# Sharing the last weighted additions of an expert layer among three engines, with larger load pieces

## The chip, the cores and the metric

The kernel runs on one core of a Trainium2 chip. The metric is the device time of one execution in microseconds. Three executions of the kernel before took 713.89, 716.54 and 720.88 us; the median is 716.54 us.

## The reference

Four layers run over 16 batches of 128 tokens with 256 features, all in float32; each adds its result to `x`:

```
x = x + long_convolution_attention(layernorm(x), ctx)      # L0_xattn
x = x + dense_plus_top2_low_rank_experts(layernorm(x))     # L0_ffn
x = x + cross_attention_16_heads_quantized(layernorm(x), ctx)   # L1_xattn
x = x + moe(layernorm(x))                                  # L1_ffn
```

Only the last one matters here. It routes every token to K = 4 of 32 experts and adds a shared expert:

```
scores = sqrt(softplus(flat @ router_w.T))
_, idx = top_k(scores + expert_bias, 4)
topv   = take(scores, idx); topv = topv / (sum(topv) + 1e-20)
probs  = zeros(T, E) with topv at idx
out    = sum over experts e of probs[:, e] * swiglu_e(flat)
out    = out + shared_swiglu(flat)
x      = x + out
```

So each token's output is its `x`, plus the shared expert's row, plus four expert rows, each with a weight of its own.

## The kernel before, in words

`build` writes one program for each engine: `tensor_program`, `vector_program`, `scalar_program`, `gpsimd_program` and `sync_program` (which issues most DMAs). Up to the routing, each program is one loop over ticks; the tables `T_PE`, `T_DVE` and so on say at which tick each step of each batch stands in the program. Nothing of that is touched by the change.

**Routing.** For each token and each of its four experts, the token's normalized row is scattered by GpSimd (L1318) into `expert_rows` in DRAM, sorted by expert. A row is 260 floats: 256 values and, in column 256, the number of the row of `y_rows` where the expert's result has to go. These numbers come from the array `dest`, made on the host: before, `512 + 2048 * k + 128 * b + p` for the k-th expert of token p of batch b.

**Expert loop.** NT = 95 tiles of 128 sorted rows go through a software pipeline. SyncE loads the tile (L1393), TensorE transposes it (L598, L599), multiplies it by the gate and up weights (L610), VectorE clamps and multiplies (L990, L992, L997), ScalarE does tanh and the copies out of PSUM (L1221, L1226, L1231, L1236), TensorE multiplies by the down weights (L583), and GpSimd scatters the 128 result rows of 1 KB into `y_rows` (L1328). GpSimd counts each landed scatter up in `s_st`; its loop ends with the waits for the landings of the last three scatters. A token's four experts are numbered so that k = 3 is the one whose tile comes first, and k = 0 the one that comes last.

**Weighted additions.** At the end every token's four rows come back. In `sync_program` (L1398 to L1406), 16 loads of 512 KB each read the rows of four batches for one k: m = 0 to 3 are the four groups of four batches for k = 3, m = 4 to 7 for k = 2, and so on. Each group g has one buffer `rb[g]`. Before the first load of a round SyncE waits until all tiles of that k have landed (`s_st` against `last[k]`), and from the second round on before each load until the four additions that read this buffer are done (`s_fin`, L1404). In DRAM a load reads 1 KB for each partition and batch:

```
o = DUMP + NB * 128 * k + 512 * g
sp.dma_start(rb[g], Yr[o:o + 512, :].rearrange("(b p) d -> p b d", p=128)).then_inc(d_r[g], 16)
```

VectorE does all 64 additions in the same order after its expert loop (L1044 to L1054): `xs[:, b, :] += rb[g][:, i, :] * weight`, as one scalar_tensor_tensor of 128x256. The weights `pk4` are made during the expert loop. ScalarE and GpSimd have nothing to do after their expert loops.

**Output.** After the 16 loads SyncE issues the 16 stores of 128 KB, batch by batch, each when the batch's last addition is done (L1410), then waits for all of them.

Of the kernel before, what the change touches and what calls it, by code (L numbers as in the profile page):

```python
# [10 lines left out]
ALU = mybir.AluOpType  # L11
ACT = mybir.ActivationFunctionType
AX = mybir.AxisListType

NB = 16
NE = 32
KT = 4
# [13 lines left out]
OFF = {}  # L31
# [22 lines left out]
SD = 32  # L54
NR = 14
DUMP = 512
NX = 12
WR = 16
NW = -(-NT // 4)
# [36 lines left out]
def build(nc, a_x, a_ctxT, a_tk, a_pack, a_qp, a_rows, a_w, a_dest, a_pad, out):  # L96
    ctx = ExitStack()
    with ctx:
        def sb(name, shape, dt=F32):
            return ctx.enter_context(nc.sbuf_tensor(name, shape, dt))  # L100

        def sem(name):
            return ctx.enter_context(nc.semaphore(name))

        xs = sb("xs", [128, NB, 256])
        tk = sb("tk", [128, 16, 256])
        pk = sb("pk", [128, NPACK])
# [17 lines left out]
        def cutter(base):  # L125
            used = [0]

            def carve(shape, dt=F32):
                n = int(np.prod(shape[1:])) // (2 if dt == BF16 else 1)
                v = base[0:shape[0], used[0]:used[0] + n]  # L130
                used[0] += n
                assert used[0] <= base.shape[1], used[0]
                if dt == BF16:
                    v = v.bitcast(BF16)
                if len(shape) == 3:
                    v = v.rearrange("p (a b) -> p a b", a=shape[1])
                if len(shape) == 4:
                    v = v.rearrange("p (a b c) -> p a b c", a=shape[1], b=shape[2])
                return v
            return carve  # L140
# [33 lines left out]
        rb = [carve([128, 4, 256]) for _ in range(4)]  # L174
        cmp_ = rb[0][:, 0, 0:NE * Q].rearrange("p (q e) -> p q e", e=NE)
        cmd_ = rb[0][:, 1, 0:NE * Q].rearrange("p (q e) -> p q e", e=NE)
        carve = cutter(tk[:, 8:16, :].rearrange("p a b -> p (a b)"))
        th = [carve([128, 2, 128]) for _ in range(3)]
        hT = [carve([128, 128]) for _ in range(2)]
# [42 lines left out]
        key = sb("key", [128, NB, 8])  # L222
        ixl = sb("ixl", [128, NB, KT], U32)
        stage = sb("stage", [128, NS, ROW])

        carve = cutter(tk[:, 6:8, :].rearrange("p a b -> p (a b)"))
        scan = carve([128, 2, NE])
# [8 lines left out]
        pk4 = tk[:, 5, 192:256].rearrange("p (b k) -> p b k", k=KT)  # L236
# [5 lines left out]
        Yr = nc.dram_tensor("y_rows", (DUMP + KT * NB * 128, 256), F32, kind="Internal").ap()  # L242

        d_in = [sem(f"d_in{g}") for g in range(len(LOADS))]
# [9 lines left out]
        d_r = [sem(f"d_r{i}") for i in range(4)]  # L254
        s_tm, s_t5, s_thr, s_x5P, s_x5 = (sem(n) for n in ("s_tm", "s_t5", "s_thr", "s_x5P", "s_x5"))
        d_xr = [sem(f"d_xr{i}") for i in range(2)]
        d_out = sem("d_out")

        v_own, p_own, a_own = (sem(n) for n in ("v_own", "p_own", "a_own"))
        s_const, s_pconst, s_st = (sem(n) for n in ("s_const", "s_pconst", "s_st"))  # L260
# [26 lines left out]
        po = ctx.enter_context(nc.psum_tensor("po", [128, 512], F32))  # L287
        gbanks, xbanks, ybanks = banks.tiles[0:3], [banks.tiles[3], cbanks.tiles[0]], sbanks.tiles
        place = banks.place

        T_PE = {"wsc": 555, "xnTA": 235, "uT": 574, "xnTB": 757, "h": 780, "rl": 802, "pa": 811, "wxp": 831,
# [322 lines left out]
        def vector_program(dve):  # L614
# [36 lines left out]
            for c in range(2):  # L651
                i = dve.tensor_scalar(bkm[:, c, :], P("par"), cols[:, 2 + c:3 + c], None, ALU.mult)
            i.then_inc(s_const, 1)

            for t in range(TICKS):
# [41 lines left out]
                for n in at(t, T_DVE["xA"], 128, 2 * NP):  # L697
                    r, co = n // 2, n % 2
# [69 lines left out]
                for n in at(t, T_DVE["z"], 32, 8 * NP):  # L768
                    r, k = n // 8, n % 8
# [10 lines left out]
                for b in at(t, T_DVE["oi"], 128, NB):  # L780
                    m = sm[b % 4]
# [10 lines left out]
                for m in at(t, T_DVE["mx"], 32, 4 * NB):  # L792
                    b, g = m // 4, m % 4
# [249 lines left out]
            dve.wait_ge(s_routed, 1)  # L1043
            for m in range(4 * KT):  # L1044
                g, k = m % 4, KT - 1 - m // 4
                dve.wait_ge(d_r[g], 16 * (m // 4 + 1))
                for i in range(4):
                    b = 4 * g + i
                    if m < 4:
                        dve.wait_ge(s_acc, b + 1)  # L1050
                    else:
                        dve.wait_ge(s_fin, 4 * (m - 4) + i + 1)
                    dve.scalar_tensor_tensor(out=xs[:, b, :], in0=rb[g][:, i, :], scalar=pk4[:, b, k:k + 1], in1=xs[:, b, :],
                                             op0=ALU.mult, op1=ALU.add).then_inc(s_fin, 1)  # L1054

        def scalar_program(act):
# [159 lines left out]
            for t in range(NT + 6):  # L1216
# [15 lines left out]
                for n in at(t, 5, 1, NT):  # L1232
# [2 lines left out]
                    act.wait_ge(s_yp, n + 1)  # L1235
                    act.activation(y[n % 4], ybanks[n % 2][:, 0:256], ACT.Copy).then_inc(s_y, 1)  # L1236

        def gpsimd_program(pool):
            own = Count(p_own)

# [81 lines left out]
            for n in range(NT + 3):  # L1322
# [3 lines left out]
                if n < NT:  # L1326
# [2 lines left out]
                        out=Yr, out_offset=bass.IndirectOffsetOnAxis(ap=xg[n % NX][:, 256:257].bitcast(U32), axis=0),  # L1329
                        in_=y[n % 4], in_offset=None).then_inc(d_sc[n % 4], 16)  # L1330

        def sync_program(sp):
            xv = a_x.rearrange("b d l -> d b l")
            sp.dma_start(pk[:, 0:NID], a_pack[:, 0:NID]).then_inc(d_id, 16)
# [63 lines left out]
            for m in range(4 * KT):  # L1398
                g, k = m % 4, KT - 1 - m // 4
                if g == 0:  # L1400
                    sp.wait_ge(s_st, last[k])
                    sp.sem_inc(s_thr, 1)
                if m >= 4:
                    sp.wait_ge(s_fin, 4 * (m - 4) + 4)  # L1404
                o = DUMP + NB * 128 * k + 512 * g
                sp.dma_start(rb[g], Yr[o:o + 512, :].rearrange("(b p) d -> p b d", p=128)).then_inc(d_r[g], 16)  # L1406
            ov = out.rearrange("b d l -> d b l")
            for b in range(NB):
                sp.wait_ge(s_fin, NB * (KT - 1) + b + 1)
                sp.dma_start(ov[:, b, :], xs[:, b, :]).then_inc(d_out, 16)  # L1410
            sp.wait_ge(d_out, 16 * NB)

# [76 lines left out]
```

## Time and profile before

| | |
|---|---|
| median of three executions | 716.54 us |
| profiled execution: time | 718.01 us |
| profiled execution: span from first to last instruction | 716.2 us |
| TensorE busy | 576.0 us (80%) |
| VectorE busy | 482.3 us (67%) |
| ScalarE busy | 379.7 us (53%) |
| GpSimd busy | 374.1 us (52%) |
| mean granted TensorE clock | 0.93 |
| the 64 weighted additions | from 683.4 to 712.1 us |

Busy shares are averages over stages with different limits. The span has a part before the expert loop, the expert loop (about 531 to 690 us), and the tail of weighted additions and stores. In the names of the profile, PE is TensorE, DVE is VectorE, ACT is ScalarE, POOL is GpSimd, SP is SyncE; SPq, ACTq and POOLq are the DMAs that these engines issue. `work<-y_rows` are the loads of the weighted additions, `y_rows<-tk,work` the scatters of the expert results.

### The profile page before, as it was taken

How to read it: one execution, taken by the hardware profiler on the slowest of the kernel's cores; microseconds unless marked ns; L12 is line 12 of the kernel's file. 1: busy time of each engine (PE TensorE's matmuls, PEld its weight loads, DVE VectorE, ACT ScalarE, POOL GpSimd, SP SyncE). 2: the span in 40 equal slices, each digit the busy share in tenths (PEclk: the TensorE clock that was granted, in tenths of full speed). 3: DMA queues.
4: the chain of work that ended last, by engine and by line, in shares of the span. 5: the costliest groups of instructions: out<-in, count | busy, mean ns of one | idle time of the engine just before them, and what ended most of it. 6: DMA issues, size and time to landing. Idle time of an engine off the chain costs nothing.

```text
span 716.2 us, 14275 instructions
## 1 busy us (share of the span) xinstructions
PE 576.0 (80%) x4045; PEld 464.6 (65%) x4045; DVE 482.3 (67%) x1462; ACT 379.7 (53%) x1107; POOL 374.1 (52%) x526
## 2 busy tenths in 40 slices
PE   1588899999997899968898689954089999999920
PEld 1487788788776777847776466642068877877810
DVE  1646747777889767869566876677247776555587
ACT  1002456756775466754467856663046666666610
POOL 6757747565382483795226512145615555555550
PEclk9999999999999999988899989995579999999975
DMA  7989999999999972232215981178545555555688
GB/s 276 228 249 334 335 335 334 330 328 318 326 309 320 312 257 72 67 121 69 60 43 156 345 307 53 55 237 308 166 119 162 163 157 158 158 160 158 206 279 289
DMA packets 135741, 155.02 MB, mean 216 GB/s; under 512 B 15249, under 2 KB 124945, under 8 KB 135409
## 3 DMA queue, kind: packets, MB, share of 16 engines
q1 hardware_dynamic: 117536, 122.50, 56.8%
q0 software_dynamic: 7632, 20.98, 8.1%
q10 hardware_dynamic: 10496, 10.62, 4.7%
q8 instruction: 36, 0.59, 0.3%
q14 instruction: 41, 0.33, 0.1%
HBM read 53.92 MB, written 100.28 MB: 215 GB/s over the span
## 4 chain that ended last, share of the span: by engine, by line
PE 60%; DVE 16%; DMA 8%; POOL 7%; issue 5%; ACT 3%; SPq 0%; ACTq 0%; DVEq 0%; POOLq 0%
PE ps L610 11%; PE pc L562 11%; PE pS L583 6%; PE pS L542 4%; POOL arena L1304 4%; PE ps L353 3%; PE ps L528 3%; DMA work<-y_rows 2%; PE po L513 2%; DMA expert_rows<-stage,ixl 2%; DMA stage<-xn_rows 2%; PE ps L483 2%; PE ps L406 2%; PE ps L393 2%; PE ps L397 2%
## 5 line engine op out<-in xcount | busy, mean ns | idle before, releaser
L1328 POOL DMA_INDIRECT y_rows<-tk,work x95 | 94.1, 991 | 81.0 <-ACT tk L1236 75.4
L562 PE MATMUL pc<-arena,tk 128*128 128x128 f32 x768 | 111.6, 300 | 14.0 <-POOL arena L1304 7.3
L562 PEld LDWEIGHTS pc<-arena,tk 128*128 128x128 f32 x768 | 99.8, 207 | 26.6 <-issue 13.8
L1304 POOL TENSOR_TENSOR arena<-arena 128x512 f32<-128x512 f32 x64 | 90.3, 1428 | 19.0 <-ACT arena L1104 18.9
L610 PE MATMUL ps<-arena,work 128*128 x380 | 99.5, 385 | 0.1
L990 DVE TENSOR_SCALAR work<-ps 128x256 f32<-128x256 f32 x95 | 40.2, 423 | 68.3 <-PE ps L610 67.5
L1169 ACT ACTIVATE work<-pS,work 128x128 f32<-128x128 f32 x256 | 72.8, 371 | 10.8 <-DVE work L796 10.8
L1318 POOL DMA_INDIRECT expert_rows<-stage,ixl x64 | 63.6, 993 | 23.8 <-issue 16.6
L610 PEld LDWEIGHTS ps<-arena,work 128*128 128x128 f32 x380 | 65.8, 193 | 5.8 <-issue 0.5
L583 PE MATMUL pS<-arena,tk 128*128 x190 | 59.6, 395 | 2.2 <-ACT tk L1226 2.1
L796 DVE TENSOR_REDUCE work<-pS 128x4 f32<-128x512 f32 x64 | 43.9, 686 | 25.3 <-PE pS L542 25.2
L778 DVE TENSOR_TENSOR arena<-pc,arena 128x512 f32<-128x512 f32 x64 | 43.5, 679 | 23.8 <-PE pc L562 23.7
L1221 ACT ACTIVATE tk<-work 128x128 f32<-128x128 f32 x95 | 29.5, 311 | 55.6 <-DVE work L990 50.8
L1244 POOL TENSOR_TENSOR stD<-stD,epsc 128x1 f32<-128x1 f32 x16 | 3.0, 190 | 87.3 <-DVE stD L623 87.3
L528 PE MATMUL ps<-pk,work 128*128 128x128 f32 x256 | 39.4, 277 | 3.5 <-ACT work L1169 1.5
L583 PEld LDWEIGHTS pS<-arena,tk 128*128 128x128 f32 x190 | 28.3, 188 | 19.4 <-issue 11.5
L1161 ACT ACTIVATE work<-ps 128x512 f32<-128x512 f32 x64 | 37.8, 591 | 3.0 <-PE ps L528 1.6
L1236 ACT ACTIVATE tk<-pS 128x256 f32<-128x256 f32 x95 | 37.0, 389 | 4.2 <-DMA y_rows<-tk,work 4.2
L542 PE MATMUL pS<-arena,work 32*128 32x256 f32 x256 | 36.2, 400 | 0.2 <-ACT work L1154 0.2
L528 PEld LDWEIGHTS ps<-pk,work 128*128 128x128 f32 x256 | 30.0, 142 | 7.2 <-issue 2.1
L353 PE MATMUL ps<-pk,arena 128*128 128x128 f32 x256 | 34.1, 282 | 0.0
L1244 POOL TENSOR_TENSOR stB<-stB,epsc 128x1 f32<-128x1 f32 x16 | 3.0, 190 | 59.1 <-DVE stB L623 59.1
(271 smaller groups left out, 1393.7 us busy)
## 6 DMA issues: line engine op xcount, KB each, us to landing
expert_rows<-stage SPq DMA_DIRECT2D x32, 2080.0 KB, 21.3
work<-expert_rows SPq DMA_DIRECT2D x95, 130.0 KB, 2.1
arena<-in_w SPq DMA_DIRECT2D x8, 1536.0 KB, 13.8
stage<-xn_rows SPq DMA_DIRECT2D x64, 130.0 KB, 2.4
xn_rows<-xnD ACTq DMA_DIRECT2D x16, 512.0 KB, 6.3
work<-y_rows SPq DMA_DIRECT2D x16, 512.0 KB, 5.3
tk<-in_tk SPq DMA_DIRECT2D x1, 2048.0 KB, 9.3
out<-xs SPq DMA_DIRECT2D x16, 128.0 KB, 2.9
```

The lines of the kernel that those rows point to most:

```text
L353: i = pe.matmul(pv, zv[:, k, :], ident, is_transpose=True, start=False, stop=(k == 7))
L528: i = pe.transpose(p[:, 128 * k:128 * k + 128], Pt[m % 3][:, 128 * k:128 * k + 128], ident)
L542: i = pe.matmul(p[:, 256 * c:256 * c + 256], qT[b % 3][r, 128 * c:128 * c + 128], kz[b % 3][r, c, :, :].rearrange("p a b -> p (a b)"), sta ...
L562: i = pe.matmul(pv, tk[:, h, 128 * d:128 * d + 128], kvv[:, ci, :, :].rearrange("p b (i h j) -> p (b i) h j", i=8, h=8)[:, :, hl, :], star ...
L583: i = pe.matmul(p[U * k:U * k + U, 0:256], hT[n % 2][:, U * k:U * k + U], arena[:, 512:][:, bass.ds(e, 256)], start=True, stop=True)
L610: i = pe.matmul(p[U * k:U * k + U, 0:256], xgT[n % 3][:, 128 * c + U * k:128 * c + U * k + U], arena[:, 256 * c:][:, bass.ds(e, 256)], sta ...
L778: dve.tensor_tensor(zv, cbanks.place["conv", n][:, :].rearrange("p (k h j) -> p k h j", h=4, j=8), x1, ALU.mult).then_inc(s_z, 1)
L796: dve.tensor_reduce(mx[:, g, :], sbanks.place["S", m][:, :].rearrange("p (k m) -> p k m", k=4), AX.X, ALU.max, negate=True).then_inc(s_mx, 1)
L1169: i = act.activation(Pt[m % 3][:, 128 * k:128 * k + 128], sbanks.place["S", m][:, 128 * k:128 * k + 128], ACT.Exp, bias=mx[:, g, k:k + 1])
L1304: pool.tensor_tensor(kv[kk % 4][:, c, half, :].rearrange("p (i h j) -> p i h j", h=8, i=8), i0, i1, ALU.mult).then_inc(s_kv, 1)
L1318: pool.indirect_dma_start(out=Xs, out_offset=bass.IndirectOffsetOnAxis(ap=ixl[:, b, k:k + 1], axis=0), in_=stage[:, j % NS, :], in_offset= ...
L1328: pool.indirect_dma_start(out=Yr, out_offset=bass.IndirectOffsetOnAxis(ap=xg[n % NX][:, 256:257].bitcast(U32), axis=0), in_=y[n % 4], in_o ...
```

## The change

It has four parts.

1. Batches 13, 14 and 15 are no longer added by VectorE (`NV = 13`), which now does 52 additions in four rounds of 13. For these three batches ScalarE multiplies the loaded row by its weight, in place, and counts up `s_part`; GpSimd then adds it to `xs` and counts up `s_fin2`. Both do so after their expert loops, in the order of the rounds: 12 multiplications and 12 additions.
2. The last four batches (group 3) have a buffer of their own for each round, `late[0]` to `late[3]`: `rb[3]`, two pieces of the space of weights that are no longer used, and the staging space. Their loads have no wait for additions. They stand in SyncE's program where they stood.
3. The rows of `y_rows` are numbered `512 + 2048 * k + 16 * p + b`. The four batches of a group are then neighbours for each token, and each load has one piece of 4 KB for each partition.
4. The stores of batches 0 to 7 are issued by SyncE, those of batches 8 to 15 by ScalarE, after its multiplications.

The semaphores `s_fin2` and `s_part` are two that were in use earlier (`s_co`, `s_wx`, each at 16 by then), and `d_late` three of the input loads' (each at 48).

```diff
+NV = 13
@@ build
+        late = [rb[3], *(pk[:, OFF["W"][0] + 1024 * i:OFF["W"][0] + 1024 * i + 1024].rearrange("p (b d) -> p b d", d=256)
+                         for i in range(2))]
+        late.append(stage[:, :, :].rearrange("p s d -> p (s d)")[:, 0:1024].rearrange("p (b d) -> p b d", d=256))
+        d_late = [(d_r[3], 0), (d_in[0], 48), (d_in[1], 48), (d_in[2], 48)]
+        s_fin2, s_part = s_co, s_wx
@@ vector_program
             for m in range(4 * KT):
                 g, k = m % 4, KT - 1 - m // 4
-                dve.wait_ge(d_r[g], 16 * (m // 4 + 1))
-                for i in range(4):
+                y4 = rb[g] if g < 3 else late[m // 4]
+                if g < 3:
+                    dve.wait_ge(d_r[g], 16 * (m // 4 + 1))
+                else:
+                    dve.wait_ge(d_late[m // 4][0], d_late[m // 4][1] + 16)
+                for i in range(min(4, NV - 4 * g)):
                     b = 4 * g + i
                     if m < 4:
                         dve.wait_ge(s_acc, b + 1)
                     else:
-                        dve.wait_ge(s_fin, 4 * (m - 4) + i + 1)
-                    dve.scalar_tensor_tensor(out=xs[:, b, :], in0=rb[g][:, i, :], scalar=pk4[:, b, k:k + 1], in1=xs[:, b, :],
+                        dve.wait_ge(s_fin, NV * (m // 4 - 1) + b + 1)
+                    dve.scalar_tensor_tensor(out=xs[:, b, :], in0=y4[:, i, :], scalar=pk4[:, b, k:k + 1], in1=xs[:, b, :],
                                              op0=ALU.mult, op1=ALU.add).then_inc(s_fin, 1)
@@ scalar_program, at its end
+            act.wait_ge(s_routed, 1)
+            for r in range(KT):
+                k, (done, base) = KT - 1 - r, d_late[r]
+                act.wait_ge(done, base + 16)
+                for b in range(NV, NB):
+                    act.activation(late[r][:, b - 12, :], late[r][:, b - 12, :], ACT.Copy,
+                                   scale=pk4[:, b, k:k + 1]).then_inc(s_part, 1)
+            ov = out.rearrange("b d l -> d b l")
+            for b in range(NB // 2, NB):
+                if b < NV:
+                    act.wait_ge(s_fin, NV * (KT - 1) + b + 1)
+                else:
+                    act.wait_ge(s_fin2, NB + (NB - NV) * (KT - 1) + b - NV + 1)
+                act.dma_start(ov[:, b, :], xs[:, b, :]).then_inc(d_out, 16)
@@ gpsimd_program, at its end
+            for r in range(KT):
+                for i, b in enumerate(range(NV, NB)):
+                    if r == 0:
+                        pool.wait_ge(s_acc, b + 1)
+                    else:
+                        pool.wait_ge(s_fin2, NB + (NB - NV) * (r - 1) + i + 1)
+                    pool.wait_ge(s_part, NB + (NB - NV) * r + i + 1)
+                    pool.tensor_tensor(xs[:, b, :], xs[:, b, :], late[r][:, b - 12, :], ALU.add).then_inc(s_fin2, 1)
@@ sync_program
-                if m >= 4:
-                    sp.wait_ge(s_fin, 4 * (m - 4) + 4)
-                o = DUMP + NB * 128 * k + 512 * g
-                sp.dma_start(rb[g], Yr[o:o + 512, :].rearrange("(b p) d -> p b d", p=128)).then_inc(d_r[g], 16)
+                if m >= 4 and g < 3:
+                    sp.wait_ge(s_fin, NV * (m // 4 - 1) + 4 * g + 4)
+                o = DUMP + NB * 128 * k
+                dst, done = (rb[g], d_r[g]) if g < 3 else (late[m // 4], d_late[m // 4][0])
+                sp.dma_start(dst, Yr[o:o + NB * 128, :].rearrange("(p b) d -> p b d", b=NB)[:, 4 * g:4 * g + 4, :]).then_inc(done, 16)
             ov = out.rearrange("b d l -> d b l")
-            for b in range(NB):
-                sp.wait_ge(s_fin, NB * (KT - 1) + b + 1)
+            for b in range(NB // 2):
+                sp.wait_ge(s_fin, NV * (KT - 1) + b + 1)
                 sp.dma_start(ov[:, b, :], xs[:, b, :]).then_inc(d_out, 16)
             sp.wait_ge(d_out, 16 * NB)
@@ kernel
-    dest[:, 0] = 512 + np.arange(KT * NB * 128)
+    dest[:, 0] = 512 + np.arange(KT * NB * 128).reshape(KT, 128, NB).transpose(0, 2, 1).reshape(-1)
```

## Rows read from the trace of the kernel before

**Rows 1.** Chain of waits, 670 to 717 us: start, length, what.
```profile
676.01 6.59 DMA y_rows<-tk,work
685.15 4.86 DMA work<-y_rows
691.73 6.28 DMA work<-y_rows
704.48 5.87 DMA work<-y_rows
```

**Rows 2.** Timeline of VectorE, its tail: start, length, instruction [idle before <-releaser].
```profile
683.44 6.43 DVE L1053 SCALAR_TENSOR_TENSOR xs<-work,tk,xs 128x256 f32<-128x256 f32 x16
690.03 1.67 DVE L1053 SCALAR_TENSOR_TENSOR xs<-work,tk,xs 128x256 f32<-128x256 f32 x4 [0.16 <-DMA work<-y_rows]
...
695.97 1.67 DVE L1053 SCALAR_TENSOR_TENSOR xs<-work,tk,xs 128x256 f32<-128x256 f32 x4 [0.47 <-DMA work<-y_rows]
698.03 11.34 DVE L1053 SCALAR_TENSOR_TENSOR xs<-work,tk,xs 128x256 f32<-128x256 f32 x28 [0.39 <-DMA work<-y_rows]
710.38 1.67 DVE L1053 SCALAR_TENSOR_TENSOR xs<-work,tk,xs 128x256 f32<-128x256 f32 x4 [1.00 <-DMA work<-y_rows]
```

**Rows 3.** Timeline of SyncE's DMA issues: start, length, instructions from there on.
```profile
699.73 5.11 SPq L1406 DMA_DIRECT2D work<-y_rows  x4
...
713.03 0.44 SPq L1410 DMA_DIRECT2D out<-xs  x1
```

**Rows 4.** Windows (last: PE clock, DMA share, GB/s); DMA queue at 405:410 us (packets, MB).
```profile
692.00:700.00 8.00, 0.00 (x0) 0.00 (x0) 6.92 (x17) 0.00 (x0) 1.10 (x2) 0.50 1.05 355
405.00:410.00 5.00, 4.02 (x35) 3.00 (x28) 4.52 (x15) 4.67 (x12) 3.78 (x5) 1.00 1.03 403
...
q1 hardware_dynamic: 626, 1.87, 96.1%
```

**Rows 5.** GpSimd's scatters, their queue at 697.5:698 us, all VectorE additions (L1053: ns min/median/max).
```profile
681.46 1.07 POOL L1328 DMA_INDIRECT y_rows<-tk,work  x1 [2.81 <-ACT tk L1236]
...
692.74 0.96 POOL L1328 DMA_INDIRECT y_rows<-tk,work  x1 [0.59 <-issue]
...
q0 software_dynamic: 1, 0.00, 0.1%
...
L1053 DVE SCALAR_TENSOR_TENSOR xs<-work,tk,xs x64: 472/480/489, 683.4 to 711.6; 128x256 f32<-128x256 f32 x64
```

**Rows 6.** By line: duration ns min/median/max, first and last start us.
```profile
L1311 POOL TENSOR_TENSOR xs<-xs,rows x16: 715/729/822, 91.6 to 465.7; 128x256 f32<-128x256 f32 x16
...
L1145 ACT ACTIVATE work<-ps,work x16: 474/475/502, 74.4 to 441.1; 128x256 f32<-128x256 f32 x16
...
L1085 ACTq DMA_DIRECT2D xn_rows<-xnD x16: 366/367/387, 118.8 to 484.8; - x16
```

**Rows 7.** VectorE and GpSimd, timelines at 60 and 308 us; three lines' durations.
```profile
308.45 1.96 DVE L709 SCALAR_TENSOR_TENSOR arena<-arena 64x128 f32<-64x128 f32 x1 [1.45 <-ACT arena L1116]
310.90 2.26 DVE L805 TENSOR_TENSOR xs<-xs,work 128x256 f32<-128x256 f32 x1
60.82 1.42 DVE L735 SCALAR_TENSOR_TENSOR lg<-rows,lg,ones 128x2 f32<-128x2 f32 x1
60.81 1.41 POOL L1304 TENSOR_TENSOR arena<-arena 128x512 f32<-128x512 f32 x1
308.82 1.43 POOL L1304 TENSOR_TENSOR arena<-arena 128x512 f32<-128x512 f32 x1
311.44 1.42 POOL L1304 TENSOR_TENSOR arena<-arena 128x512 f32<-128x512 f32 x1
...
L709 DVE SCALAR_TENSOR_TENSOR arena<-arena x16: 272/274/1955, 58.3 to 413.8; 64x128 f32<-64x128 f32 x16
...
L805 DVE TENSOR_TENSOR xs<-xs,work x16: 425/426/2259, 115.8 to 481.6; 128x256 f32<-128x256 f32 x16
...
L1304 POOL TENSOR_TENSOR arena<-arena x64: 1391/1422/1552, 9.4 to 317.9; 128x512 f32<-128x512 f32 x64
```

## The prediction

> **What bounds the kernel now.** I read the chain of waits of the last 46 us first, since the change touches nothing before about 673 us. In it the weighted additions stand between three loads of 4.86, 6.28 and 5.87 us [rows 1]; ahead of it runs the expert loop, which TensorE bounds and the change leaves alone. The reader is to see that the chain alternates between VectorE and the DMA queue: VectorE empties a buffer, SyncE reloads it, VectorE meets it again three buffers later.
>
> The timeline of VectorE gives the sizes [rows 2]. 16 additions take 6.43 us, so the step is (6.43 - 0.48) / 15 = 0.397 us, and a batch group of four 1.6 us. From 690.03 to 695.97 three groups take 5.94 us, 1.98 each: there the loads set the pace. From 698.03 on 28 additions run through, and only the last group waits again, 1.00 us. So VectorE (64 x 0.397 = 25.4 us of 28.6) and the transfers are both nearly full, and taking work from VectorE alone gives back only what the loads allow. The issue times of the loads [rows 1, 3] show why: each goes out when its group of the round before is done (691.73 = 690.03 + 1.67 + 0.03, and 699.73 = 698.03 + 1.67 + 0.03), none waits for a scatter.
>
> **Part 1: 12 of 64 additions leave VectorE.** A round falls from 16 to 13 additions, 6.4 to 5.15 us; four rounds save 4.8 us of VectorE. Without anything else in the way I lay it out. Round 1 begins at 683.44 as now and ends at 688.6 (13 x 0.397). The first load of round 2 still waits for the fourth addition (685.15) and lands at 690.0 as now: of the 1.25 us saved, all is lost to that wait.
>
> **Part 2: loads in pieces of 4 KB.** Now the pieces are 1 KB, and with the queues full they move 355 GB/s [rows 4]. No row has 4 KB pieces. The nearest has 3 KB ones (the expert weights): 403 GB/s at the same full share [rows 4]. I take 403 against 355, so 512 KB cost 1.30 us in place of 1.48, and a load behind others is spaced 1.98 x 355/403 = 1.74 us. Bounds: no gain (355), or 5% over 403. In the piece of weight traffic 626 packets carry 1.87 MB, so pieces of 3 KB are not cut up; that the 4 KB are cut would cost 0.2 us a load. The Trainium skill speaks against the gain: "DMA: Bandwidth & Descriptors", section Bandwidth, puts a core's limit for HBM to SBUF at about 358 GB/s, which would leave the pace as it is and the sum some 1.2 us higher (seven loads from 698 on, 0.18 us each). The trace disagrees with that limit: its 403 GB/s stand beside it.
>
> Round 2 then has its groups at 690.0, 691.7, 693.4 and the single addition from 695.2 to 695.6. Round 3's loads go out at 691.6, 693.3, 695.0 and at once after it; they land behind the last scatters, at about 697.0, 698.7, 700.2 and 701.5. VectorE ends its groups at 698.6, 700.3, 701.9 and 702.3.
>
> **Part 3: own places for the last group.** Its loads have no wait on VectorE but stand in SyncE's program behind the load of the third group, which has one. So they go out 0.4 us behind it, not earlier. Round 4 may start when the last scatter has landed; that is issued at 692.74 and its queue's last packet falls in the half microsecond from 697.5 [rows 5]. VectorE's 698.6 comes after it, so the load goes out at 698.6 in place of 699.73. The others follow at 700.3, 701.9 and 702.3 in place of 704.48 [rows 1]. The very last, behind three others, takes 5.2 us (now 5.87): it lands at 707.5, not 710.35: **-2.85 us**.
>
> **Part 4: what follows the last landing.** Now 5.87 us: four additions and the stores, the last issued at 713.03 and the span ending 3.19 us later [rows 3]. Afterwards ScalarE first multiplies three batches, 0.475 us each by the nearest scaled copy [rows 6], so 1.43 us; only then come its eight stores, because batches 8 to 15 stand behind the multiplications in its program. An issue costs 0.37 us on ScalarE [rows 6]. GpSimd's three additions, 0.73 us each, are ready 0.48 + 2.2 = 2.7 us after the landing, before the issues reach batch 13 (1.43 + 5 x 0.37 = 3.3). So the last issue begins at 1.43 + 7 x 0.37 = 4.0, and with 3.19 behind it the stretch is 7.2 us: **+1.3 us**. SyncE's eight stores (batches 0 to 7) are out before that. Behind ScalarE's new waits stand these stores alone, behind GpSimd's nothing, so no other engine waits for either. The new row numbers in y_rows cost nothing that I can find: a scatter writes 128 rows of 1 KB one by one either way, beside a TensorE that bounds the loop; without that cover a slower one would show as in rival C.
> Sum without interference: -2.85 + 1.3 = -1.5 us.
>
> **Part 5: GpSimd and VectorE at the same time.** This is the cost that I think decides. GpSimd can't begin its 12 additions before its own loop is over, that is at the landing of the last scatter, 698. Six of them (rounds 1 and 2, multiplied long before by ScalarE, idle from 690) then run without a gap: 6 x 0.73 = 4.4 us [rows 6], just while VectorE has round 3. What two such instructions do to each other is seen in the attention phase [rows 7]. A VectorE scalar_tensor_tensor with its inputs in SBUF, 0.27 us as a rule, took 1.96, and an addition with two inputs there, 0.43 as a rule, took 2.26; in both cases GpSimd ran a tensor_tensor meanwhile (308.82 to 310.25 and 311.44 to 312.86), and VectorE ended 0.16 and 0.30 us after it. At 60.8 both began together and VectorE's instruction on 2 columns ended 0.02 us after GpSimd's. Meanwhile none of GpSimd's 64 instructions of 1.42 us went over 1.55. So VectorE waits for GpSimd and not the other way. The Trainium skill has this as a rule ("SBUF — State Buffer", Who interferes with whom): a VectorE instruction with two SBUF inputs and a GpSimd one that reads SBUF share an exclusive port, and the second fully blocks; by that the two engines' times add. Trace and rule agree there; what the tail itself shows is weaker, since the 64 additions stayed at 472 to 489 ns beside GpSimd's indirect DMAs [rows 5], which are no tensor_tensor.
>
> Price: the blocked 4.4 us fall on the third group of round 3, so the last two loads go out 4.4 us later, and so does the last landing. Bounds: zero if they don't meet, and 12 x 0.73 = 8.8 us if every GpSimd addition stands in VectorE's way on the chain. If VectorE keeps the port instead, GpSimd's 8.8 us shift behind: VectorE is done at 708.6, GpSimd's rest (8.8 less some 2 us of gaps) by 715.4, the last store 0.4 + 3.2 us later, 719.0. Both orders come out within a microsecond; I take 4.4.
> Sum: -1.5 + 4.4 = +2.9 us. The profiled execution has span 716.2 and time 718.0, so 720.9 in its own terms; it is 1.5 us above the median of 716.54, and I put the same difference on the median: **719.4 us**.
>
> **Rivals.**
> A, no meeting: -1.5 us, 715.0. For it: no row has this very pair; VectorE idles about 1 us in round 4 anyway and GpSimd could fit in. Against it: rows 7.
> B, slower: every GpSimd addition shuts VectorE out, because six then three come back to back and each finds VectorE between two instructions; with 8.8 us on the chain it is 716.54 - 1.5 + 8.8 = 723.8. It decides from about 8.5 us of blocking on, which needs round 3's three additions to hit before the third group is done as well. Against it: those wait for a landing at about 701.5 and for ScalarE, and the last three meet at most five additions of VectorE.
> C, the 4 KB pieces hold up the scatters. Now a scatter issued at 676.01 takes 6.59 us beside four loads [rows 1] and GpSimd stands 2.81 us [rows 5]. If the scatters get a smaller share, the loop ends up to 1.5 us later and the last scatter too: 717 without blocking, 721 with it. Against it: the burst itself gets shorter.
> D, the pieces bring more than 13% and nothing meets: the last landing can't come before 3.67 MB have moved from 698 on, at 420 GB/s 706.7, so 714 at the best. Faster by over 1% would need 709.4 and isn't in reach of the mechanism; it is left to the scatter of the runs.
>
> **How the numbers follow.** A measurement of this kernel can tell about 1%, 7.2 us, from no change; three runs of before lie 7 us apart. Chances: the forecast (717.5 to 722) 0.50, A 0.24, B 0.11, C 0.12, D 0.03. The forecast, A and D lie inside 1%; B lies at its edge and I count most of it as slower, C a little by the runs' scatter. So faster 0.03, same 0.83, slower 0.14. The range reaches from A less 1.5 us of scatter, 713.5, to B, 723.8: 8 in 10.
>
> **What would show it.** Right: VectorE's additions after 698 with some of 0.8 us and more, or gaps between them that end with GpSimd's additions; the last load of y_rows landing near 712; ScalarE's last store issued 4 us after that. Wrong on the blocking: all 52 additions at 0.48 us with a step of 0.40, and the last landing at 707 to 708. Wrong on the pieces: spacing of loads still 1.98 us. Wrong on the stores: the last store is released by GpSimd's addition, not by the issue before it. The forecast fails upward if the last landing comes after 715 and downward if before 709.

## The result, and the profile after

| | before | changed |
|---|---|---|
| median, 18 executions each on the same chips | 718.31 us (712.93 to 723.38) | 726.98 us (719.57 to 730.62) |
| ratio | | 1.011, 95% interval 1.008 to 1.0141 |
| profiled execution: time, span | 718.01, 716.2 us | 730.21, 728.4 us |

The changed kernel is slower by 1.1%, some 8 us; the forecast was 719.4 us, 2.9 us above the 716.54 us of before, with a range up to 723.8. (In this comparison the kernel before has a median 1.8 us higher, 718.31 us.) Executions of either kernel spread over 10 us, for the most part ahead of the tail: the first scatter into `y_rows` falls anywhere from 528.5 to 543.4 us in the profiles below. So I count all times of the tail from that scatter (532.19 us before, 533.72 changed). The span from there is 184.0 us before and 194.7 changed: **10.7 us lost in the tail**, the other 1.5 us of the 12.2 between the spans lie ahead of it. Single profiles still differ in the tail by about 1 us: the kernel with one late memset (below) has the program of before up to the last addition of VectorE, and that addition ends 178.8 us after the first scatter, in place of 179.9.

The timeline of VectorE in the changed kernel (start, length, instruction, idle time before it and who ended it) answers to [rows 2]:

```profile
684.61 5.23 DVE L1064 SCALAR_TENSOR_TENSOR xs<-work,tk,xs 128x256 f32<-128x256 f32 x13
690.25 1.67 DVE L1064 SCALAR_TENSOR_TENSOR xs<-work,tk,xs 128x256 f32<-128x256 f32 x4 [0.41 <-DMA work<-y_rows]
693.91 1.67 DVE L1064 SCALAR_TENSOR_TENSOR xs<-work,tk,xs 128x256 f32<-128x256 f32 x4 [1.98 <-DMA work<-y_rows]
696.08 1.67 DVE L1064 SCALAR_TENSOR_TENSOR xs<-work,tk,xs 128x256 f32<-128x256 f32 x4 [0.49 <-DMA work<-y_rows]
698.98 0.48 DVE L1064 SCALAR_TENSOR_TENSOR xs<-pk,tk,xs 128x256 f32<-128x256 f32 x1 [1.23 <-DMA pk<-y_rows]
700.36 8.84 DVE L1064 SCALAR_TENSOR_TENSOR xs<-work,tk,xs 128x256 f32<-128x256 f32 x12 [0.89 <-DMA work<-y_rows]
709.13 0.47 DVE L1064 SCALAR_TENSOR_TENSOR xs<-pk,tk,xs 128x256 f32<-128x256 f32 x1
709.52 3.26 DVE L1064 SCALAR_TENSOR_TENSOR xs<-work,tk,xs 128x256 f32<-128x256 f32 x8
715.78 1.67 DVE L1064 SCALAR_TENSOR_TENSOR xs<-work,tk,xs 128x256 f32<-128x256 f32 x4 [2.99 <-DMA work<-y_rows]
717.37 0.48 DVE L1064 SCALAR_TENSOR_TENSOR xs<-stage,tk,xs 128x256 f32<-128x256 f32 x1
```

Two things are to be seen. VectorE has 12 additions less and waits 8.0 us for loads in place of 2.5. And the 12 additions from 700.36 take 8.84 us; at the old step of 0.397 they would take 4.85. GpSimd's timeline shows what stands beside them, and ScalarE's shows the end:

```profile
693.63 0.95 POOL L1354 DMA_INDIRECT y_rows<-tk,work  x1 [1.66 <-DMA y_rows<-tk,work]
700.10 2.45 POOL L1365 TENSOR_TENSOR xs<-xs,work 128x256 f32<-128x256 f32 x3 [5.51 <-ACT pk L1254]
702.51 5.22 POOL L1365 TENSOR_TENSOR xs<-xs,pk 128x256 f32<-128x256 f32 x6
717.75 2.08 POOL L1365 TENSOR_TENSOR xs<-xs,stage 128x256 f32<-128x256 f32 x3 [10.02 <-ACT stage L1254]
```

```profile
717.10 0.51 ACT L1254 ACTIVATE stage<-stage,tk 128x256 f32<-128x256 f32 x1 [11.63 <-DMA stage<-y_rows]
717.11 0.85 ACTq L1262 DMA_DIRECT2D out<-xs  x2
717.52 0.89 ACT L1254 ACTIVATE stage<-stage,tk 128x256 f32<-128x256 f32 x2
718.00 2.98 ACTq L1262 DMA_DIRECT2D out<-xs  x6
```

The last load is that of group 3 into `stage`. SyncE's timeline and the DMA view (KB, us from issue to landing) have it:

```profile
709.59 0.43 SPq L1442 DMA_DIRECT2D stage<-y_rows  x1
...
stage<-y_rows SPq DMA_DIRECT2D x1, 512.0 KB, 7.5
```

So it lands at 717.1, where ScalarE begins to multiply. The load that VectorE waits for at 715.78 is the last but one.

All stores are issued by 721 and landed by 722.8. What then holds the span open until 728.4 stands in the lines of the closing barrier, at the kernel's end (L98 before, L99 changed: instruction, duration in ns min/median/max, first and last start in us). Each engine has one DRAIN there, an instruction that the engine's queue carries out behind the engine's own work. Before:

```profile
L98 POOLq DRAIN  x1: 8322/8322/8322, 698.3 to 698.3; - x1
L98 SPq DRAIN  x1: 7/7/7, 716.0 to 716.0; - x1
```

Changed:

```profile
L99 POOLq DRAIN  x1: 9658/9658/9658, 718.5 to 718.5; - x1
L99 SPq DRAIN  x1: 7/7/7, 722.8 to 722.8; - x1
L99 POOLq EVENT_SEMAPHORE  x2: 17/17/17, 728.2 to 728.3; - x2
```

SyncE's DRAIN comes when the last store has landed. GpSimd's closing DRAIN takes 8.3 us (the 9.66 us of the changed kernel include the last 1.3 us of the additions that end at 719.83). Before, it ran from 698.3 to 706.6 under VectorE's additions and nobody met it. Now its 8.3 us count from the end of GpSimd's last addition, it ends at 728.2, and it is the end of the kernel, 5.4 us after the stores. The busy rows of the page don't count a DRAIN, so neither page shows it.

The 10.7 us, from the first scatter on: last load landed 183.4 in place of 178.2 (+5.2); from there to the last store landed 5.7 in place of 5.6 (+0.1); from there to the end 5.6 in place of 0.2 (+5.4).

### The profile page after: what moved, and what is told of

The parts are those of the page before. It is cut to its first block, busy times and chain, and to the rows that moved or that the text cites. A ratio compares the mean times of both kernels' runs of the same rounds, so it can differ in the third digit from the quotient of the medians.

```text
span 728.4 us, 14300 instructions
## 1 busy us (share of the span) xinstructions
PE 577.9 (79%) x4045; PEld 465.2 (64%) x4045; DVE 480.8 (66%) x1450; ACT 384.3 (53%) x1119; POOL 382.1 (52%) x538
## 4 chain that ended last, share of the span: by engine, by line
PE 60%; DVE 17%; POOL 7%; issue 6%; DMA 5%; ACT 3%; POOLq 0%; SPq 0%; ACTq 0%; DVEq 0%
PE ps L617 12%; PE pc L569 10%; PE pS L590 6%; PE pS L549 4%; POOL arena L1330 3%; PE ps L535 3%; DMA work<-y_rows 3%; PE ps L360 2%; PE po L520 2%; PE ps L490 2%; POOL expert_rows L1344 2%; PE ps L413 2%; PE ps L400 1%; DVE xs L1064 1%; PE ps L404 1%
```

## The experiments

My theory after this reading: (D) the DRAIN, (L) GpSimd's additions slow VectorE's, (P) the pieces of 4 KB are slower, because the transfers from 701 to 711 us had a low rate (172 GB/s at a share of 0.57). Later (W): the removal of additions from VectorE brings nothing since the loads take its place. The edits are shortened to the lines that matter.

**Pieces of 4 KB alone.** `dest` and the load as in the change, everything else as before:

```diff
-                o = DUMP + NB * 128 * k + 512 * g
-                sp.dma_start(rb[g], Yr[o:o + 512, :].rearrange("(b p) d -> p b d", p=128)).then_inc(d_r[g], 16)
+                o = DUMP + NB * 128 * k
+                sp.dma_start(rb[g], Yr[o:o + NB * 128, :].rearrange("(p b) d -> p b d", b=NB)[:, 4 * g:4 * g + 4, :]).then_inc(d_r[g], 16)
```

> Only the pieces: the kernel before with the new row numbers and the loads in 4 KB pieces, 16 KB apart in DRAM from partition to partition; all 64 additions stay on VectorE, the four buffers and SyncE's 16 stores too. Theory P (pieces at this distance are slower): in the changed kernel a load took 6.0 to 8.4 us to land while the queues were loaded and the windows show 129 GB/s at a share of 0.49, which is 263 at a full share against 355 before. Then the load intervals grow from 1.98 to 2.3 us or more and the time rises by 2 to 5 us. Rival (the loads were late only because VectorE was held up): no load interval above 2.0 us, time 1 us below to 1 us above before. The view of the blueprint forecast (403 GB/s): 1 to 2 us faster.

Measured: ratio 0.9998 (0.9955 to 1.0042). Neither the loss of theory P nor the gain that I had forecast for the pieces is seen: the last addition ends 180.4 us after the first scatter, in place of 179.9. The interval is 3 us wide on either side, so the times alone exclude a loss of more than 3 us, and not my gain of 1 to 2.

**Pieces of 4 KB, contiguous loads** (the load's `rearrange` is changed to match, `(p b) d -> p b d` with b = 4):

```diff
-    dest[:, 0] = 512 + np.arange(KT * NB * 128)
+    dest[:, 0] = 512 + np.arange(KT * NB * 128).reshape(KT, NB // 4, 128, 4).transpose(0, 1, 3, 2).reshape(-1)
```

> The same 4 KB pieces, but the rows numbered so that the 512 KB of a load are contiguous in DRAM (group, token, batch in the group): pieces 4 KB apart and not 16 KB. Everything else as before. Theory P1 (the distance of 16 KB costs, not the size): the intervals fall to about 1.7 us and the time is 1 to 2 us below before, 3 us or more below the kernel with 16 KB distance. Theory P2 (large pieces themselves cost, for instance by an uneven share among the 16 engines): as slow as with 16 KB distance, within 1 us. Rival (neither matters): all three within 1 us.

Measured: 0.9996 (0.9952 to 1.004). Neither size nor distance of the pieces matters for the time here within 0.4%. The rates are less flat. Two windows of this kernel (the last three columns are TensorE's granted clock, the DMA engines' busy share, GB/s):

```profile
703.00:705.00 2.00, 0.00 (x0) 0.00 (x0) 1.80 (x5) 0.00 (x0) 1.15 (x1) 0.50 1.02 416
705.00:707.00 2.00, 0.00 (x0) 0.00 (x0) 2.00 (x6) 0.00 (x0) 0.00 (x0) 0.50 1.03 401
```

So with pieces of 4 KB the queues did move 400 GB/s at a full share, for 4 us (one scatter is among the loads). Over 22 to 24 us of loads the three kernels move 313 (before, share 0.96), 299 (4 KB, 0.89) and 298 GB/s (contiguous, 0.86); divided by the share, an estimate, that is 326, 336 and 347. The DMA engines are a little less busy per byte, but the time doesn't fall by anything that shows.

**A late instruction on GpSimd.**

```diff
+            pool.wait_ge(s_fin, 4 * KT * 4)
+            pool.memset(nhalf[:, :], -0.5)
```

> The kernel before with one more GpSimd instruction: a memset of one column, after a wait for the 64th addition. It moves the end of GpSimd's program from 698 to 712 us and does nothing else. Theory D (GpSimd's closing DRAIN, 8.3 us from 698.3 before and 9.7 us from 718.5 in the changed kernel, always lasts 8 to 10 us once indirect DMAs were issued, and is shown once it starts late): it starts at 712 and ends at 720 to 722, so the time rises by 4 to 6 us. Rival (the DRAIN waits for something that the scatters or VectorE's additions leave behind, and is short when these are long over): the time stays within 1 us.

Measured: 723.43 against 718.32 us, ratio 1.0067 (1.0025 to 1.0108), 4.8 us. GpSimd's timeline and the barrier's lines of this kernel:

```profile
712.95 0.10 POOL L1332 MEMSET nhalf<- 128x1 f32 x1 [14.26 <-DVE xs L1053]
```

```profile
L98 POOLq DRAIN  x1: 8447/8447/8447, 712.9 to 712.9; - x1
L98 SPq DRAIN  x1: 7/7/7, 716.8 to 716.8; - x1
```

A memset of one column costs 4.8 us, since the DRAIN behind it ends at 721.4, 4.6 us after the stores. Theory D is shown by itself. That the indirect DMAs ahead of it are what makes the DRAIN long isn't shown: no kernel here goes without them.

**A DRAIN ahead of GpSimd's additions**, in the changed kernel:

```diff
+            pool.drain()
             for r in range(KT):
                 for i, b in enumerate(range(NV, NB)):
```

> The changed kernel with a drain instruction on GpSimd between its scatter loop and its 12 additions. Theory D1 (the closing DRAIN's 8.3 us are work left over from the indirect DMAs, done once): the first DRAIN takes 8.3 us at about 700, the additions come after it and the closing one is short, under 1.5 us; the time falls by 3 us or more against the changed kernel. Theory D2 (any DRAIN on GpSimd takes 8 us, or the last one does whatever went before): both take 8 us, and the time rises by 2 to 6 us.

Measured: 1.0073 (1.0035 to 1.0111). The two DRAINs (L1358 and L99) and GpSimd's additions:

```profile
L1358 POOLq DRAIN  x1: 8322/8322/8322, 711.0 to 711.0; - x1
```

```profile
719.46 2.53 POOL L1366 TENSOR_TENSOR xs<-xs,work 128x256 f32<-128x256 f32 x3 [13.53 <-issue]
721.95 5.04 POOL L1366 TENSOR_TENSOR xs<-xs,pk 128x256 f32<-128x256 f32 x6
726.95 2.08 POOL L1366 TENSOR_TENSOR xs<-xs,stage 128x256 f32<-128x256 f32 x3
```

```profile
L99 POOLq DRAIN  x1: 2069/2069/2069, 727.0 to 727.0; - x1
```

The first DRAIN takes the 8.322 us, and the closing one 2.07, which is the last three additions (2.08) that it waits for. So the 8.3 us are paid once, by the first DRAIN behind the scatters: D1. Part of the gain is lost again, since the additions now wait for this DRAIN: they start 13.53 us after GpSimd's last scatter instruction, in place of 5.51. Against the changed kernel the gain is 0.4% by the two ratios, whose intervals overlap, so the 3 us that I expected aren't shown by the times. In its one profile the span from the first scatter is 188.0 us in place of 194.7.

**GpSimd's tensor_tensor beside VectorE's additions**, in the kernel before, on scratch tiles:

```diff
+            for n in range(12):
+                if n >= 3:
+                    pool.wait_ge(own.sem, own.n - 2)
+                pool.tensor_tensor(stage[:, n % 3, 0:256], stage[:, 4, 0:256], stage[:, 5, 0:256],
+                                   ALU.add).then_inc(*own.up())
```

> The kernel before, with 12 GpSimd tensor_tensor instructions of 128x256 on scratch tiles behind its scatter loop; they touch nothing that VectorE or a DMA uses, and nobody waits for them. Theory L (a GpSimd instruction that reads SBUF holds up VectorE's additions, which have two inputs there): VectorE's additions stop or stretch for about 12 x 0.70 = 8.4 us in total, the loads that wait for them go out later, and VectorE's last addition is 4 to 8 us later, counted from the first scatter into y_rows (179.9 us before). Rival (the two engines don't hinder each other): the additions keep their 0.40 us step and the last one stays within 1.5 us of 179.9. GpSimd's DRAIN then starts near 707 and may show by 0 to 2 us in either case.

**The same with memsets** (14 of 600 columns):

```diff
+                pool.memset(flat[:, 600 * (n % 3):600 * (n % 3) + 600], 0.0).then_inc(*own.up())
```

> The same place, but 14 GpSimd memsets of 600 columns, about 0.6 us each: as long in total, writing SBUF and reading nothing. Theory L with the rule that only a reading GpSimd instruction hinders: VectorE's additions keep their step of 0.40 us, last addition within 1.5 us of 179.9 after the first scatter. Rival (any GpSimd work on SBUF hinders VectorE): as in the run with tensor_tensor.

VectorE and GpSimd with tensor_tensor:

```profile
710.49 16.81 DVE L1053 SCALAR_TENSOR_TENSOR xs<-work,tk,xs 128x256 f32<-128x256 f32 x28 [0.34 <-DMA work<-y_rows]
...
710.43 10.24 POOL L1334 TENSOR_TENSOR stage<-stage 128x256 f32<-128x256 f32 x12 [4.60 <-DMA y_rows<-tk,work]
```

and with memsets:

```profile
704.36 13.34 DVE L1053 SCALAR_TENSOR_TENSOR xs<-work,tk,xs 128x256 f32<-128x256 f32 x32 [0.47 <-DMA work<-y_rows]
...
708.97 7.61 POOL L1335 MEMSET stage<- 128x600 f32 x14 [4.65 <-DMA y_rows<-tk,work]
```

Before, 28 additions took 11.34 us [rows 2]; beside 12 tensor_tensors they take 16.81, 5.5 us more or 0.46 for each. VectorE ends 186.0 us after the first scatter in place of 179.9. Beside memsets the step is (13.34 - 0.48) / 31 = 0.415 us, 0.02 above the old one. The durations say it more sharply: the 12 additions beside tensor_tensors last 939 to 955 ns, the 20 beside memsets 476 to 484, as those alone. The times are 1.0068 (1.0027 to 1.0108) and 1.0012 (0.9972 to 1.0052). So theory L holds and it is the reading that hinders, as the Trainium skill says ("SBUF — State Buffer", Who interferes with whom: two SBUF inputs on VectorE contend with a GpSimd instruction that reads SBUF, not with one that only writes it). The same section calls the shared port pair an exclusive lock, and says of VectorE's two-port modes that the engine that comes second fully blocks for the whole instruction. That is not what the changed kernel shows for this pair: there GpSimd's six from 702.51 take 0.87 us each (5.22 / 6), and VectorE's beside them begin at 702.75, 703.62, 704.48 and 705.35, the same step; it is less than 0.40 + 0.69 (2.08 / 3, GpSimd alone) = 1.09. They alternate and overlap in part, and **both** are slowed (GpSimd's last from 0.72 to 0.90 us, VectorE's from 0.48 to 0.94).

**The changed kernel with NV = 16.**

```diff
-NV = 13
+NV = 16
```

> The changed kernel with NV = 16: VectorE does all 64 additions again, ScalarE multiplies nothing and GpSimd adds nothing; own places, 4 KB pieces 16 KB apart and the stores from two engines stay (ScalarE still waits for the last load before its eight stores). By theory D and by the held-up VectorE (12 of its additions took 8.84 us in place of 4.9 beside GpSimd) the GpSimd additions cost 5.4 + 4 us less the 4.8 us that VectorE saves: this kernel is then 4 to 5 us faster than the changed one, and slower than before by what the pieces cost. Rival (the pieces are the whole loss): no faster than the changed kernel.

Measured: 720.08 us, ratio 1.0047 (1.0012 to 1.0082). That is 4.5 us below the changed kernel by the ratios, as expected for the GpSimd part, and 3.4 us (0.9 to 5.9) above before. The pieces don't explain that rest. Its profile has the tail at 184.2 us, as before, and no line for it. Part of it may be chance: the mean granted clock was 0.937 or more in seven of the 35 executions of before, which took 711 to 713 us, and at most 0.933 in the 12 of this kernel, the shortest of which took 718.18. Own places or the stores from two engines are left besides, and which it is stays open.

**TensorE in place of GpSimd**, in the changed kernel: GpSimd's additions removed, SyncE storing batches 0 to 11 and ScalarE the other four, and

```diff
+            for r in range(KT):
+                for i, b in enumerate(range(NV, NB)):
+                    pe.wait_ge(s_part, NB + (NB - NV) * r + i + 1)
+                    pe.matmul(gbanks[i][:, 0:256], ident, late[r][:, b - 12, :], start=(r == 0), stop=(r == KT - 1)).then_inc(s_fin2, 1)
@@ vector_program
+                dve.tensor_tensor(xs[:, b, :], gbanks[i][:, 0:256], xs[:, b, :], ALU.add).then_inc(s_fin, 1)
```

> The changed kernel without the 12 GpSimd additions: ScalarE multiplies as in the change, TensorE (idle since 688) adds up the four scaled rows of batches 13 to 15 in PSUM by multiplying with the identity, and VectorE adds each sum to xs once, so it does 55 additions instead of 64. SyncE stores batches 0 to 11, ScalarE 12 to 15. GpSimd's program ends with its scatters. If the lock on VectorE and the late DRAIN are the whole loss of the change, this is at least as fast as NV = 16 (720.1) and 7 us or more faster than the changed kernel, and 0 to 3 us faster than before, since VectorE has 9 additions (3.6 us) less. Rival (VectorE's additions were not the limit, the landing of the last scatter and the loads are): within 1 us of before.

Measured: 1.0037 (1.0001 to 1.0074). That is 5.2 us below the changed kernel by the ratios, less than the 7 that I expected, and 2.7 us (0.1 to 5.4) above before, so the rival (within 1 us) wasn't met either. GpSimd's DRAIN is hidden again (706.1 to 714.4 of 726.5 us) and no addition is slowed, and still it is no faster than before. VectorE's waits say why: seven for loads, 7.0 us in all, and three more for TensorE's sums at the end, 2.2 us. The longest of each kind:

```profile
701.55 3.45 DVE L1069 SCALAR_TENSOR_TENSOR xs<-work,tk,xs 128x256 f32<-128x256 f32 x8 [2.09 <-DMA work<-y_rows]
...
722.18 0.42 DVE L1074 TENSOR_TENSOR xs<-ps,xs 128x256 f32<-128x256 f32 x1 [1.33 <-PE ps L624]
```

That led to theory W.

**52 additions and nothing in their place** (batches 13 to 15 lack their expert rows; the counts in the waits follow):

```diff
-                for i in range(4):
+                for i in range(min(4, 13 - 4 * g)):
```

> The kernel before in which batches 13 to 15 get no expert rows at all (their 12 additions are left out, so those three batches lack the expert layer's weighted sum). VectorE does 52 additions with nobody else working beside it; loads of 1 KB pieces, four buffers, 16 stores by SyncE, as before. Forecast of mine: VectorE's saving of 4.8 us shows by 2.85 us at the last landing. Theory W (each load waits for its buffer, and with 13 additions a round the wait for the transfer grows by what VectorE saves): the span of the additions stays at 28.6 us within 1 us, and the time within 1.5 us of before. Rival (VectorE sets the pace): additions end 3 to 5 us earlier, time 3 to 4 us below before.

Measured: 725.10 against 724.64 us, ratio 1.0008 (0.9973 to 1.0042). Twelve additions less bring nothing that the times show; a gain of up to 2 us isn't excluded, the 4.8 us are. VectorE's timeline:

```profile
689.13 5.24 DVE L1053 SCALAR_TENSOR_TENSOR xs<-work,tk,xs 128x256 f32<-128x256 f32 x13
695.02 1.67 DVE L1053 SCALAR_TENSOR_TENSOR xs<-work,tk,xs 128x256 f32<-128x256 f32 x4 [0.66 <-DMA work<-y_rows]
698.00 1.67 DVE L1053 SCALAR_TENSOR_TENSOR xs<-work,tk,xs 128x256 f32<-128x256 f32 x4 [1.30 <-DMA work<-y_rows]
700.22 2.26 DVE L1053 SCALAR_TENSOR_TENSOR xs<-work,tk,xs 128x256 f32<-128x256 f32 x5 [0.55 <-DMA work<-y_rows]
703.35 5.46 DVE L1053 SCALAR_TENSOR_TENSOR xs<-work,tk,xs 128x256 f32<-128x256 f32 x13 [0.86 <-DMA work<-y_rows]
709.63 3.26 DVE L1053 SCALAR_TENSOR_TENSOR xs<-work,tk,xs 128x256 f32<-128x256 f32 x8 [0.81 <-DMA work<-y_rows]
713.99 2.07 DVE L1053 SCALAR_TENSOR_TENSOR xs<-work,tk,xs 128x256 f32<-128x256 f32 x5 [1.10 <-DMA work<-y_rows]
```

The idle times add up to 5.3 us, 2.8 more than before. The last addition ends 179.3 us after the first scatter (716.06 - 536.72) against 179.9: 0.5 us of the 4.8. From the first addition to the last it is 26.9 us against 28.6, 1.7 less, so the 1 us that theory W allowed was exceeded; here the first addition itself came 1.2 us later. The last store lands 184.4 us after the first scatter, 0.6 later than before: the DMA engines are full from 694 to 711 us (share 1.02) and, with the stores, on to 719 (0.99).

**Own places for all loads of rounds 2 to 4**, in the space of the expert weights, from TensorE's last tile on; no load waits for VectorE:

```diff
+        for j in range(12):
+            done, at0 = (d_in[j], 48) if j < 6 else (d_xn[j - 6], 16 * NB // 2) if j < 8 else (d_r[j - 8], 16)
+            rs.append((arena[:, 1024 * j:1024 * j + 1024].rearrange("p (b d) -> p b d", d=256), done, at0))
@@ sync_program
-                if m >= 4:
-                    sp.wait_ge(s_fin, 4 * (m - 4) + 4)
+                if m == 4:
+                    sp.wait_ge(s_yp, NT)
```

> The kernel before with places of their own for all 12 loads of rounds 2 to 4, in the space of the expert weights, from the moment when TensorE is done with them: no load waits for VectorE. 64 additions on VectorE, pieces of 1 KB, 16 stores by SyncE. Theory W: rounds 2 and 3 are loaded when VectorE comes to them, so its additions run with almost no gap until round 4, which waits for the last scatter; the additions end 1 to 3 us earlier and the time is 1 to 3 us below before. Rival (the transfers themselves, 340 GB/s shared with the scatters, set the pace, or the loads now hold up the last scatters): within 1 us of before, or later.

Measured: 1.0015 (0.998 to 1.0051). The rival holds, and of the 1 to 3 us that I expected only the lowest part stays within the interval.

```profile
691.51 6.42 DVE L1059 SCALAR_TENSOR_TENSOR xs<-work,tk,xs 128x256 f32<-128x256 f32 x16
700.43 19.42 DVE L1059 SCALAR_TENSOR_TENSOR xs<-arena,tk,xs 128x256 f32<-128x256 f32 x48 [2.50 <-DMA arena<-y_rows]
```

Now 48 additions run through without a gap, but they begin 2.5 us late, because the loads go out only when TensorE is done. The waits are gathered at one place.

**Both together**, own places and 52 additions (batches 13 to 15 again lack their expert rows):

> Both: own places for rounds 2 to 4 and only 52 additions (batches 13 to 15 lack the expert rows again). It shows what fewer additions are worth once no load waits for VectorE. Theory W: 3 us or more below the kernel before, 1 to 3 us below the one with own places and 64 additions. Rival (last scatter and round 4's 2 MB set the end): within 1 us of the one with 64 additions.

Measured: 1.0017 (0.9979 to 1.0055); no gain either. The first and the last of VectorE's stretches in its timeline:

```profile
697.11 3.26 DVE L1059 SCALAR_TENSOR_TENSOR xs<-arena,tk,xs 128x256 f32<-128x256 f32 x8 [2.88 <-DMA arena<-y_rows]
...
710.70 5.24 DVE L1059 SCALAR_TENSOR_TENSOR xs<-arena,tk,xs 128x256 f32<-128x256 f32 x13 [0.79 <-DMA arena<-y_rows]
```

The window over that stretch (the last three columns are TensorE's granted clock, the DMA engines' busy share, GB/s):

```profile
694.00:711.00 17.00, 0.00 (x0) 0.00 (x0) 11.17 (x28) 0.00 (x0) 2.18 (x3) 0.57 1.03 339
```

Round 4 is there at 710.70 though nothing waits for VectorE, and the DMA engines are full all the way, at 339 GB/s [rows 4 have 355]. In the changed kernel the share from 686 to 717 us is 0.76. So W was only half right: the loads take the place of VectorE, but with VectorE's hold on them gone the transfers alone fill the same time. One rival is left: with own places the first load of round 2 waits for TensorE's last tile and goes out 155.8 us after the first scatter (156.0 with 64 additions) in place of 153.0, and from 689 to 694 us the DMA share is 0.25. Whether loads that start at the old time would gain those 3 us, or only slow the last scatters, no run here tests.

**Stores in turn by two engines**, with own places: even batches by SyncE, odd ones by ScalarE.

> Own places for rounds 2 to 4 and 64 additions, with the stores issued in turn by SyncE (even batches) and ScalarE (odd batches). SyncE's last store goes out 1.0 us after the last addition before; with two engines it can go out 0.1 us after it. Theory: 0.5 to 1 us below the one with stores by SyncE alone. Rival (the last transfers share the engines anyway): no difference.

Measured: 723.39 us, 0.9991 (0.9957 to 1.0026) against before, 0.24% below the one with SyncE alone, not separable. No version of mine is faster than the kernel before by more than the noise.

## Why the prediction was wrong

Point by point, with the tail counted from the first scatter:

- **Missing term: GpSimd's closing DRAIN, +5.4 us.** The sum ended at the landing of the last store. In part 4 I said that behind GpSimd's new waits stands nothing; there stood the DRAIN of 8.3 us. The trace of before held it; I had looked at GpSimd's instructions, whose last is at 692.74, and not at the lines of the barrier. This one step takes the result out of the range: 726.98 less 5.4 is 721.6, below 723.8.
- **Parts 1 to 3, forecast -2.85 us at the last landing.** Failed. VectorE's 12 fewer additions alone bring 0.5 us at the last addition, within the spread of single profiles, and none in the time. I had spaced the loads by 1.74 us with a rate of 403 GB/s that pieces of 4 KB would reach; the pieces alone change the time by nothing that shows (0.9998), and the intervals of the round-2 groups are 3.66 and 2.17 us, the single addition 2.90 later. The 403 GB/s were measured on another transfer, the weights, at another place. The contiguous loads come near it in single windows, but over the tail no kernel keeps it.
- **Part 3, the very last load.** I gave it 5.2 us behind three others. It took 7.5, sent out at the same moment as the one before it (709.59 and 709.23) since it has no wait of its own. Why it took that long isn't shown.
- **Part 5, the slowed VectorE, forecast +4.4 us.** Right that VectorE is slowed by GpSimd's additions, and right in size: 12 additions took 4.0 us more. The order in which I saw it wasn't: GpSimd doesn't shut VectorE out for six additions, nine of its additions run in a row (700.10 to 707.73) and alternate with VectorE's at 0.87 us. Nine times 0.46 us comes out near six times 0.73; that agreement is luck.
- The two together: forecast +1.55 for the last landing, measured +5.2. Of the 3.7 us between, 1.4 are the last load's later issue (175.9 us after the first scatter; 706.7, that is 174.5, by the forecast) and 2.3 its longer way. The measured +5.2 is the 4.0 us of VectorE less the 0.5 of the fewer additions, which leaves 1.7 us without a cause shown.
- **Part 4, from the last landing to the last store:** forecast 7.2 us, measured 5.7, so +0.1 in place of +1.3. ScalarE's issues are the last step, as forecast, but its first store is issued at 717.11, beside the first multiplication and not behind the third (I had added 1.43 us for them). The last one begins at 720.5, 3.4 us after the landing in place of 4.0, and lands 2.2 us later in place of 3.19.
- **The rivals.** B gave 723.8 by a full shut-out; the size was nearer than the forecast's, for a wrong reason. C and D did not come. A, no meeting, is excluded by the changed kernel's own additions of 0.94 us and by the run with tensor_tensor.
- Of the signs named ahead: the last landing was expected near 712 and came at 717.1, above the 715 from which I had called the forecast failed upward.

## What to carry to other kernels

Work that is given to an idle engine also moves the end of that engine's program, and what stands behind the end comes with it: on GpSimd, in these kernels full of indirect DMAs, a DRAIN of 8.3 us. Look at the lines of the closing barrier of every engine before moving work to it, and ask when its DRAIN would end. And where VectorE and the transfers are both nearly full, work taken from VectorE alone is given back to waits for the transfers (fewer bytes were not tried): leave the work out of the kernel once, which is the cheapest way to learn what moving it can bring.

## What the runs showed of the hardware that I had not expected

- GpSimd's first DRAIN behind its indirect DMAs lasts 8.322 us in ten of the profiles here, to the nanosecond, and where a GpSimd instruction still runs it is 8.3 us from that instruction's end (10.893 in the run with tensor_tensor, with 2.57 us of additions left). A second DRAIN costs nothing of its own (2.07 us, all of them spent on the last additions).
- A GpSimd tensor_tensor of 128x256 costs VectorE's two-input additions 0.46 us (12 of them 5.5 us); memsets of 128x600, 0.54 us each, cost them nothing that shows (20 additions beside 14 memsets at 476 to 484 ns).
- Executions can differ far ahead of the tail: from 300 to 380 us TensorE's mean granted clock (1 is its upper level, 2.4 GHz, and 0.5 the lower, 1.2 GHz) was 0.89 in the profiles of before and changed, and 0.96 in that of the pieces alone, whose first scatter came 3.7 us earlier than before's. Single spans are therefore no measure of a change in the tail here.
